# Two units' slots weighed in one run, and three places for the sums, in a two-layer interaction kernel

## The reference

```python
def _cin_forward(x, Ws):            # x: 512 x 39 x 64
    x0 = x
    h = x
    outs = []
    for W in Ws:                    # W0: 39 x 39 x 128, W1: 39 x 128 x 128
        h = jnp.einsum('bid,bjd,ijh->bhd', x0, h, W)
        outs.append(h)
    out = jnp.concatenate(outs, axis=1)
    return out.sum(axis=-1)         # 512 x 256
```

## Time and profile before

| | us |
|---|---|
| median of 3 runs | 304.52 (303.5 to 304.7) |
| profiled execution, its own time | 304.13 |
| its span, first to last instruction | 302.3 |
| PE busy | 262.5 (87%) |
| DVE busy | 207.8 (69%) |
| ACT busy | 176.7 (58%) |
| mean granted clock of PE | 0.949 |

### The profile page before, as it was taken

The page is one execution under the profiler, slowest core; times in us unless marked ns, Lnnn a source line. Parts: engine busy times, 40 slices in busy tenths (PEclk is TensorE's granted clock), DMA queues, the critical chain, the costliest instruction groups (busy, mean ns, idle before and its releaser), DMA issues.

```text
span 302.3 us, 16797 instructions
## 1 busy us (share of the span) xinstructions
PE 262.5 (87%) x7411; PEld 239.3 (79%) x7411; DVE 207.8 (69%) x832; ACT 176.7 (58%) x330; POOL 47.9 (16%) x125
## 2 busy tenths in 40 slices
PE   2999999919745748397999999999999999999996
PEld 2995866819744647297999989999989999999996
DVE  0298898999139999865899849989966898500000
ACT  1577777718936364445877767777758777760000
POOL 9999279400000000000000000000000000000000
PEclk9999999967999597669999999999999999999999
DMA  7910000032016565433354424535433453100000
GB/s 242 422 54 2 1 0 0 3 121 61 0 48 201 166 184 171 115 114 112 113 189 138 126 110 143 186 109 180 151 116 120 131 198 111 49 0 20 0 2 17
DMA packets 11111, 31.95 MB, mean 106 GB/s; under 512 B 1232, under 2 KB 2000, under 8 KB 10960
## 3 DMA queue, kind: packets, MB, share of 16 engines
q1 hardware_dynamic: 10512, 31.15, 31.6%
q10 hardware_dynamic: 576, 0.52, 0.5%
HBM read 31.14 MB, written 0.52 MB: 105 GB/s over the span
## 4 chain that ended last, share of the span: by engine, by line
PE 79%; DVE 8%; issue 6%; ACT 5%; DMA 1%; SPq 0%; DVEq 0%
PE out_ps L667 36%; PE stage L651 22%; PE stage L627 18%; DVE arena L446 4%; ACT arena L556 4%; DVE arena L437 3%; PE stage L636 2%; DMA arena<-in_w 1%; PE out_ps L662 1%; ACT arena L589 1%; ACT arena L564 1%; DVE arena L443 0%; DVE arena L440 0%; SPq L306 0%; SPq L305 0%
## 5 line engine op out<-in xcount | busy, mean ns | idle before, releaser
L667 PE MATMUL out_ps<-arena 128*128 (+1 forms) x920 | 111.3, 281 | 0.0
L667 PEld LDWEIGHTS out_ps<-arena 128*128 128x128 f32 x920 | 106.7, 195 | 4.4 <-issue 4.3
L651 PE MATMUL stage<-arena 64*32 64x115 f32 (+4 forms) x6144 | 83.4, 243 | 22.8 <-issue 12.3
L651 PEld LDWEIGHTS stage<-arena 64*32 64x32 f32 x6144 | 74.5, 109 | 29.4 <-issue 26.5
L446 DVE TENSOR_TENSOR arena<-arena 128x392 f32<-128x392 f32 (+5 forms) x288 | 90.3, 385 | 0.0
L589 ACT COPY arena<-stage 128x460 f32<-128x460 f32 x128 | 63.2, 545 | 36.5 <-PE stage L651 33.6
L437 DVE TENSOR_TENSOR arena<-arena 128x224 f32<-128x224 f32 (+1 forms) x192 | 58.0, 343 | 36.4 <-PE stage L651 36.3
L627 PE MATMUL stage<-arena 128*128 128x231 f32 (+2 forms) x234 | 54.1, 396 | 5.7 <-DMA arena<-in_w 5.7
L573 ACT COPY arena<-arena 128x768 f32<-128x768 f32 (+1 forms) x51 | 44.8, 884 | 23.2 <-PE out_ps L667 22.2
L627 PEld LDWEIGHTS stage<-arena 128*128 128x128 f32 x234 | 42.9, 198 | 16.6 <-issue 5.7
L351 DVE TENSOR_TENSOR arena<-arena 128x18 f32<-128x18 f32 (+26 forms) x189 | 47.1, 336 | 8.4 <-ACT arena L548 6.4
(11 more groups left out here) (13 smaller groups left out, 10.6 us busy)
## 6 DMA issues: line engine op xcount, KB each, us to landing
arena<-in_x_d SPq DMA_DIRECT2D x32, 448.0 KB, 3.8
arena<-in_x_w SPq DMA_DIRECT2D x32, 360.0 KB, 3.2
arena<-in_c SPq DMA_DIRECT2D x2, 640.0 KB, 9.9
arena<-in_w SPq DMA_DIRECT2D x1, 1152.0 KB, 8.5
arena<-in_w SPq DMA_DIRECT2D x1, 896.0 KB, 5.7
arena<-in_w SPq DMA_DIRECT2D x2, 274.5 KB, 6.0
out<-arena ACTq DMA_DIRECT2D x4, 128.0 KB, 1.7
arena<-in_w SPq DMA_DIRECT2D x1, 448.0 KB, 4.0
```

Source lines behind the costliest of these rows:

```text
L651: done = nc.tensor.matmul(banks[2 * four_place + s][WIDE * column:WIDE * (column + 1), 0:LISTED * FOUR] .rearrange("p (n b) -> p b n", b=F ...
L667: return nc.tensor.matmul(out_ps[:, 0:HID] if single else out_ps[:, HID:2 * HID], view(s_at, (1, B)), view(c_at, (1, HID)), start=False, s ...
```

## The change

PE's turn becomes: sums of the first unit; weigh the slots of two units in one run (52 records); sums of the second unit; branch. So the second unit's sums are followed, behind the branch, by the sums of the next turn's first unit. The fours of a turn go to three places in the order 0, 1, 2, 1. PE waits on `emptied` only before the second four of a unit. The part order of a pair becomes columns 0, 3, 1, 2, 0, 3. ACT stages four halves in a row ahead of the second unit of a turn (two at a batch's start), and makes the singles of two units one after the other, after the first unit of a turn, where a batch is being weighed.

```diff
+        FOUR_PLACES = [0, 1, 2, 1]
...
-            for q in range(FOURS):
-                n, t = divmod(q * FOUR, PAIRS)
-                u, v = q * FOUR // UNIT, t // UNIT
-                if n >= 1 and t == 0:
-                    act.wait_ge(emptied, emptied_through_four(q - 1))
-                if n >= 1 and t % UNIT == 0:
-                    for i, (a, b) in enumerate(HALVES):
-                        half = (n - 1) * IN_ALL + v * len(HALVES) + i
-                        stage(s0[(n - 1) % 2] + (SINGLES + v * EACH) * B, a, b, half)
-                act.wait_ge(filled, SETUP_BANKS + q + 1)
...
-                                   banks[2 * (q % 2) + s][:, 0:LISTED * FOUR].rearrange("p (n b) -> p n b", b=FOUR))\
-                        .then_inc(emptied, 1)
-                if (q + 1) * FOUR % UNIT == 0 and u + PRODS < UNITS:
-                    singles(u + PRODS)
...
+            def stage_unit(n, v):
+                for i, (a, b) in enumerate(HALVES):
+                    stage(s0[n % 2] + (SINGLES + v * EACH) * B, a, b, n * IN_ALL + v * len(HALVES) + i)
...
+            for u in range(UNITS):
+                n, v = divmod(u, IN_BATCH)
+                if n >= 1 and v == 0:
+                    act.wait_ge(emptied, emptied_through_four(u * UNIT // FOUR - 1))
+                    stage_unit(n - 1, v)
+                if n >= 1 and v % PRODS == 1:
+                    stage_unit(n - 1, v)
+                    if v + 1 < IN_BATCH:
+                        stage_unit(n - 1, v + 1)
+                    else:
+                        stage_rest(n - 1)
+                for q in range(u * UNIT // FOUR, (u + 1) * UNIT // FOUR):
+                    t = q * FOUR % PAIRS
+                    act.wait_ge(filled, SETUP_BANKS + q + 1)
+                    for s in range(2):
+                        nc.scalar.copy(view(s0[n % 2] + s * PAIRS + t, (B, LISTED), (1, FOUR)),
+                                       banks[2 * FOUR_PLACES[q % len(FOUR_PLACES)] + s][:, 0:LISTED * FOUR].rearrange("p (n b) -> p n b", b=FOUR))\
+                            .then_inc(emptied, 1)
+                if n == 0 or v % PRODS == 0:
+                    if n >= 1 and u > IN_BATCH:
+                        singles(u - 1 + PRODS)
+                    if u + PRODS < UNITS:
+                        singles(u + PRODS)
+                if n >= 1 and v == IN_BATCH - 1:
                     take_out(n - 1)
...
-            ORDER = [(0, 0), (3, 0), (0, 1), (3, 1), (1, 0), (2, 0)]
+            ORDER = [(0, 0), (3, 0), (1, 0), (2, 0), (0, 1), (3, 1)]
...
                     for half in range(2):
-                        pe.wait_ge(emptied, banks_wanted)
-                        pe.reg_add(banks_wanted, banks_wanted, 2)
-                        sum_four(v, half, half)
-                    behind(v)
+                        if half == 1:
+                            pe.wait_ge(emptied, banks_wanted)
+                            pe.reg_add(banks_wanted, banks_wanted, 4)
+                        sum_four(v, half, FOUR_PLACES[2 * v + half])
+                    if v == 0:
+                        behind()
...
-                        def weigh_unit(v):
-                            for a, b in HALVES:
-                                staged_half()
-                                weigh_staged(first + v, a, b)
-                        turn(w_wanted, unit_wanted, banks_wanted, weigh_unit)
+                        def weigh_units():
+                            for v in range(PRODS):
+                                for a, b in HALVES:
+                                    staged_half()
+                                    weigh_staged(first + v, a, b)
+                        turn(w_wanted, unit_wanted, banks_wanted, weigh_units)
```

More of the change, by code:

```diff
@@ L576, in _ @@
             IN_ALL = IN_BATCH * len(HALVES) + len(REST_HALVES)
-            for q in range(FOURS):
-                n, t = divmod(q * FOUR, PAIRS)
-                u, v = q * FOUR // UNIT, t // UNIT
-                if n >= 1 and t == 0:
-                    act.wait_ge(emptied, emptied_through_four(q - 1))
-                if n >= 1 and t % UNIT == 0:
-                    for i, (a, b) in enumerate(HALVES):
-                        half = (n - 1) * IN_ALL + v * len(HALVES) + i
-                        stage(s0[(n - 1) % 2] + (SINGLES + v * EACH) * B, a, b, half)
-                act.wait_ge(filled, SETUP_BANKS + q + 1)
-                for s in range(2):
-                    nc.scalar.copy(view(s0[n % 2] + s * PAIRS + t, (B, LISTED), (1, FOUR)),
-                                   banks[2 * (q % 2) + s][:, 0:LISTED * FOUR].rearrange("p (n b) -> p n b", b=FOUR))\
-                        .then_inc(emptied, 1)
-                if (q + 1) * FOUR % UNIT == 0 and u + PRODS < UNITS:
-                    singles(u + PRODS)
[L595 to L604, removed]
@@ new lines, in stage_unit, with stage_rest @@
+            def stage_unit(n, v):
+                for i, (a, b) in enumerate(HALVES):
+                    stage(s0[n % 2] + (SINGLES + v * EACH) * B, a, b, n * IN_ALL + v * len(HALVES) + i)
+            def stage_rest(n):
+                (a, b), (_, c) = REST_HALVES
+                half, s_at = (n + 1) * IN_ALL - len(REST_HALVES), s0[n % 2]
+                stage(s_at, a, b, half)
+                act.wait_ge(weighed, half)
+                nc.scalar.copy(view(t_0 + b * B, (1, (SINGLES - b) * B)), view(s_at + b * B, (1, (SINGLES - b) * B)))
+                nc.scalar.copy(view(t_0 + SINGLES * B, (1, (c - SINGLES) * B)),
+                               view(s_at + (SINGLES + IN_BATCH * EACH) * B, (1, (c - SINGLES) * B))).then_inc(staged, 1)
@@ L705, in _ @@
                 pe.reg_mov(unit_wanted, 1)
-                pe.reg_mov(banks_wanted, emptied_through_four(-2))
+                pe.reg_mov(banks_wanted, emptied_through_four(-1))
                 pe.reg_mov(staged_wanted, 1)
@@ L709, in _ @@
                 with pe.Fori(0, IN_BATCH // PRODS):
-                    turn(w_wanted, unit_wanted, banks_wanted, lambda v: None)
+                    turn(w_wanted, unit_wanted, banks_wanted, lambda: None)
                 pe.wait_ge(c1_ready, 1)
```

## The result

The changed kernel is slower by 0.7%: ratio 1.0071, 95% interval 1.0042 to 1.0101, from 20 executions of each, beside a forecast of +2.7 us or 0.9%. The medians are 303.47 us (301.69 to 306.43) and, beside it, 302.73 us for the kernel before (299.77 to 305.01); the ratio leaves out executions more than 1.5% above the fastest of their kernel, so it isn't the quotient of the medians, which alone would say 0.2%.

A forecast was written before the change was run, and what follows sets the result against it. The prediction took PE itself to bound the kernel, at 10.98 us per turn of two units. Terms 1.3 + 0.6 + 0.85 + 0 = +2.7 us on 304.13 gave 306.8 us, range 305.3 to 308.6, chance 0.45.

The forecast's parts named there:

- Longer weighing runs: PE's weighing: 5 runs per batch instead of 8, each run fewer saving 0.19 us at its two ends.
- joint: Where PE's runs of two units are joined, three per batch, 9 in three batches; forecast +0.15 us each, +1.3 us together.
- The joined sums: PE's sums of two units in one run: 0.21 us saved at the ends, 0.55 us lost at the branch, three times per batch.
- The list's DMA: ACT's singles wait for a list landing 1.6 us into the next turn: 0.08 us in each of 8 turns, +0.6 us.
- The one late landing: One of 8 lists landing as late as 4.7 us, holding ACT's singles: +0.85 us, bounds 0 to 2.6.
- The order of a pair: PE's new part order: taken as 0, bounds -1.5 to +1.5 us; rival 302 us if pairs get cheaper, chance 0.17.
- the same ring: Old and new part order, read cyclically, are both (0, 3)(0, 3)(1, 2), first and second parts exchanged; so taken as 0 us.
- The sign that I named for it: Fours within a run of sums seen other than 1.09 us apart would show that the order counts.
- Places: PE's second four behind the branch needs its place copied: fits by 0.3 us; without the branch a 0.2 to 0.3 us stall.
- DVE, batches' ends: DVE's products free by 1.1 us; batches' ends keep their order, with setup and first batch taken 0, bounds -1.8 and +1.8.
- rule of the drain at a change of tiling mode: A change of tiling mode drains TensorE; fewer runs by this alone give -3.6 us, 300.5 us, which the prediction excluded.
- rule on a taken branch: A branch to code outside the fetched window stalls for a DMA; at each of 9 branches 323 us, chance 0.02.

## Why the prediction was right, and where only in the sum

It forecast slower, by 2.7 us or 0.9%, with turns of 11.1 to 11.3; measured are 0.7% (2.2 us by the batches) and 11.27. Its 306.8 us stood on a median of 304.52 for the kernel before, from 3 executions; over 20 that kernel measured 302.73 and the changed one 303.47, so the difference is what can be compared, not the time. Step by step:

- **Longer weighing runs, -0.19 per joint.** A run of 52 records takes 6.05 us, not 6.00, and the rest of 22 records 2.71. Over a batch weighing fell from 7 x 3.10 + 5.57 = 27.27 us to 4 x 6.05 + 2.71 = 26.91: -0.12 per joint.
- **The joined sums, -0.21 + 0.55.** This is the term that was mis-sized. With the old order two units are 2.39 + 0.48 + 2.45 = 5.32 us around the branch (0.48 is the mean of 0.45 and 0.51 for the idle part) against 4.78: +0.54 instead of +0.34. The distance of the fours at the branch is 1.82 us, not 1.65: the sequencer needs 0.8 us from L716 to the first matmul, not 0.65, and the extra lies between the MOVE of the branch and the unit's first wait (197.6 to 197.8; 0.1 in the earlier trace rows). That the branch makes most of it and not the unit's waits was argued then and is shown now: 1.82 with, 1.30 without. With it a joint costs 0.39 us by the batches with the old order (48.77 against 47.6), where the prediction had 0.15.
- **The list's DMA, +0.6 and +0.85.** The chain was nearly right in length: a turn of 11.1 plus 0.08 forecast, 11.09 to 11.23 measured where it sets the turn. But I had added it to the joint, and it runs beside it: with the branch in place a turn takes 11.27, and by the 7.3 us plus DMA a list shows only when its DMA takes over about 3.95 us (an estimate from the four turns above). So the +0.6 was nothing in the later batches: taken away, they stay at 48.37 us. The one late landing did come, in the first weighed batch of the profiled execution, and cost PE 0.72 us, near the 0.85. Whether every execution has one is not shown.
- **The order of a pair, 0.** Wrong, by -0.4 us per batch (48.77 with the old order, 48.33 with the new), -1.3 in all, within the bound I gave. The argument that the same ring costs the same doesn't hold: a third cut of it costs 1.12 us per four. The sign that I named for it (fours other than 1.09 us apart) would have missed the gain, which lies at the ends of a run.
- **Places.** The place wait didn't show with the branch, as forecast; without it it is 0.1 us, not 0.2 to 0.3.
- **DVE, batches' ends.** Nothing new of theirs appeared in the chain of the later batches.

So the direction and the main cause, the branch between sums, were right, and that the sum came out so near is luck: nine joints cost 2.1 us more than forecast, while the order gave 1.3 and the lists' 0.6 fell away. The Trainium skill's rule of the drain at a change of tiling mode (TensorEngine Tiling (Array Packing), Key Properties) agrees with the trace: fewer changes save time. With the new order on both sides it is 10.72 against 10.82 us per turn, with the unit's waits of 0.21 us already paid out of it; the rest of the way from 10.98 is the order. The Trainium skill's rule on a taken branch (Runtime: NRT & Kernel Launch, Instruction fetch mechanics) took effect where the loop's body was doubled, with 60 code loads, not in the changed kernel, which has 11 like the one before.

What stays open: what in the array makes one cut of the ring of parts faster than another, inside a run of sums and at its ends; and how a body of two units could be had with no branch in the sums and no code outside the loop. The latter wasn't tried.

## What to carry to other kernels

A loop's branch needs work ahead of it in the engine's queue, long enough to cover the sequencer's steps: behind 26 large matmuls it was free, between small ones it cost 0.5 us each time, more than the drains that the join saved. Before two waits are added, ask whether they run side by side: here branch (11.27 us per turn) and list (11.09 to 11.23) were within 0.2 us of each other, removing the list's chain alone changed nothing in the later batches, removing the branch alone gave 0.2 us at most, and only both together, with the place wait gone too, gave 10.72. And when a change bundles edits, run each alone: the part order was the one part whose gain the traces show.

## What the runs showed of the hardware that I had not expected

- The order in which small matmuls are given to the pieces of the array moved a unit's sums from 2.31 to 2.39 and 2.42 us, with the same matmuls.
- With a loop body of two units (and its weighing) there were 11 code loads in all, and idle stretches of over 1 us in the sums only in its first pass; with one of four units 60 loads, idle stretches of up to 2.6 us at every pass, and a median 94 us higher.
- The granted clock of PE from 115 to 135 us was 0.70 in one execution and 1.00 in another of nearly the same work. In it one weighing run took 5.13 us instead of 3.10, which is as much as the whole change.
